# Attention stage of a routed transformer layer: queries and keys turned together, statistics in one pass, shared rotations, and PSUM places dealt anew (scores 3 to 2, side products 1 to 2)

## What is computed

```python
q, k, v = (split_heads(x @ w.T) for w in (wq, wk, wv))      # q and k also times 64 ** -0.25
q, k = rope(q), rope(k)                                      # pairs (x0, x1): x0*c - x1*s, x0*s + x1*c
out = softmax(q @ k.T + causal_mask) @ v
x1 = layernorm(x + merge_heads(out) @ wo.T)
stats = [mean, std, min, max, l2, share of |x1| < 1e-6]      # six numbers for each token
hidden = concat(x1, stats) @ r1_w.T                          # what the router reads
```

## Time and profile before

| | |
|---|---|
| time, median of 3 runs | 2268.77 us (2255.43, 2268.81, 2268.77) |
| the profiled execution, own time | 2260.15 us |
| its span (first to last instruction) | 2258.3 us |
| TensorE matmul busy | 1936.1 us (86%) |
| VectorE, ScalarE, GpSimd busy | 1347.9, 1040.6, 775.0 us |
| mean granted TensorE clock | 0.911 of 2.4 GHz |

### The profile page before, as it was taken

The page is one execution under the profiler, slowest core; times in us unless marked ns, Lnnn a source line. Parts: engine busy times, 40 slices in busy tenths (PEclk is TensorE's granted clock), DMA queues, the critical chain, the costliest instruction groups (busy, mean ns, idle before and its releaser), DMA issues. The chain is left out here.

```text
span 2258.3 us, 39106 instructions
## 1 busy us (share of the span) xinstructions
PE 1936.1 (86%) x13154; PEld 1727.6 (76%) x13154; DVE 1347.9 (60%) x3015; ACT 1040.6 (46%) x2293; POOL 775.0 (34%) x901
## 2 busy tenths in 40 slices
PE   5999999999999999999999999442178999999990
PEld 4778888878788878888878888341178999999980
DVE  7466554566654566554466663386885656656645
ACT  4344344444344444344444333315175666666655
POOL 1322043331043322033332000100085766766742
PEclk8799999999999999899999999555588999999995
DMA  4222122322223232222322221300004444554428
GB/s 121 69 75 76 47 73 70 90 76 78 60 73 78 77 84 75 62 61 61 90 80 83 64 66 27 139 34 0 0 14 128 137 156 141 155 172 133 143 50 298
DMA packets 154370, 198.48 MB, mean 88 GB/s; under 512 B 24612, under 2 KB 119824, under 8 KB 150124
## 3 DMA queue, kind: packets, MB, share of 16 engines
q1 hardware_dynamic: 138348, 186.33, 26.6%
q0 software_dynamic: 15872, 10.24, 2.7%
HBM read 129.65 MB, written 56.62 MB: 82 GB/s over the span
## 5 line engine op out<-in xcount | busy, mean ns | idle before, releaser
L518 PEld LDWEIGHTS out_ps<-v_sb,probs 128*128 128x128 f32 x4352 | 575.9, 197 | 30.6 <-ACT probs L642 7.3
L518 PE MATMUL out_ps<-v_sb,probs 128*128 128x65 f32 x4352 | 586.1, 275 | 3.6 <-ACT probs L642 3.3
L742 DVE TENSOR_REDUCE part_max<-rows_ps 128x1 f32<-128x512 f32 (+2 forms) x576 | 345.5, 617 | 204.1 <-PE rows_ps L474 137.0
L642 ACT ACTIVATE probs<-scores_ps 128x512 f32<-128x512 f32 (+3 forms) x640 | 329.7, 533 | 146.9 <-PE scores_ps L505 74.8
L1502 PE MATMUL up_ps<-xe_t,w 128*128 128x320 f32 x1920 | 289.8, 311 | 1.7 <-DVE xe_t L1609 1.7
L1502 PEld LDWEIGHTS up_ps<-xe_t,w 128*128 128x128 f32 x1920 | 284.6, 189 | 2.4 <-issue 1.9
L501 PE MATMUL scores_ps<-q,k_st 128*128 128x512 f32 (+2 forms) x640 | 279.3, 436 | 0.0
L474 PE MATMUL rows_ps<-k_st,q 128*128 128x512 f32 (+3 forms) x640 | 246.3, 408 | 25.3 <-DVE part_max L742 15.3
L896 POOL TENSOR_TENSOR products<-qk,cos_sin 128x256 f32<-128x256 f32 x224 | 160.2, 747 | 280.3 <-ACT qk L599 280.3
L502 PE MATMUL scores_ps<-q,k 68*128 68x512 f32 (+2 forms) x640 | 238.7, 373 | 0.0
L1465 POOL DMA_INDIRECT acc_rows<-out_rows,token x96 | 148.7, 1549 | 127.5 <-ACT out_rows L1592 116.5
(11 more groups left out here) (243 smaller groups left out, 2960.8 us busy)
## 6 DMA issues: line engine op xcount, KB each, us to landing
w_raw<-in_w_expert SPq DMA_DIRECT2D x32, 1536.0 KB, 6.5
k<-k_st SPq DMA_DIRECT2D x160, 128.0 KB, 2.3
q<-q_up_cols SPq DMA_DIRECT2D x128, 128.0 KB, 2.8
w_raw<-in_w_adapter SPq DMA_DIRECT2D x32, 384.0 KB, 7.1
x_t<-in_x_t SPq DMA_DIRECT2D x64, 128.0 KB, 2.3
q_up_cols<-q_st SPq DMA_DIRECT2D x64, 128.0 KB, 2.4
q_low_cols<-q_st SPq DMA_DIRECT2D x64, 128.0 KB, 2.5
x_row<-in_x SPq DMA_DIRECT2D x64, 128.0 KB, 2.1
```

Of the source, the lines that this page charges most:

```text
L518: mm = pe.matmul(o_ps[:, u % 2, s * (HD + 1):(s + 1) * (HD + 1)], probs[:, g % P_RING, s * P:(s + 1) * P], v_sb[:, place(b, j), h, :], sta ...
L642: act.activation(probs[:, g % P_RING, low:CH], s_ps[:, g % S_RING, low:CH], ACT.Exp).then_inc(exp_done, 1)
L742: red = dve.tensor_reduce(to, r_ps[:, e % 2, 0:width], AX.X, ALU.max, negate=g == 0)
```

## The change

1. **Turned together.** The host sets the rows of wq and wk side by side head by head, so that one transpose of 128 columns holds one head's query and key. Four transposes do for a tile instead of eight, with one copy (L664 in the new kernel) and one subtraction (L748). `dup` is gone, and `qt` and `kt` become one step `turn`. The halves that hold keys are moved into `k_st` by two DMAs for each tile, beside the two stores of queries; whoever reads those keys waits for the DMAs (`keys_stored`).
2. **Statistics in one pass.** The six numbers are copied to three blocks of 32 columns (GpSimd), so that upper and lower parts of data and weights meet in one matmul of 96 rows instead of three of 6 rows.
3. **Shared rotations.** In the front GpSimd makes the rotations of tiles 1, 4 and 7, VectorE the others; the split of `w_o` and `w_r1` moves behind tile 1.
4. **PSUM.** Two places for scores, two for side products; `claim` waits for the product two before. When chunks are over, side products use the places of scores and rows too, six in all.
5. **Order.** `x1` comes 3 slots after `wo`, `stats` one later, a new step `sparse` one later (the moments' first instruction moves into `x1`); rings of 4 for `y`, `x1` and the moments. Row work of units 1 to 3 moves from before the slots into slots 0 to 8. In a slot rows are sorted by unit, so a turn of maxima stands ahead of the next unit's row. The tail takes a tile each slot.

```diff
-S_RING = 3
+FIRST_ON_POOL = (1, 4, 7)
+S_RING = 2
+M_RING = 2
...
-        apart = 2 if i // GROUP == len(groups) - 1 else 7
+        apart = 1 if i // GROUP == len(groups) - 1 else 7
...
-                                  ("dup", 3, False), ("qt", 1, True), ("kt", 1, True)))
+                                  ("turn", 3, True)))
...
-        steps = (("ot", 0, True), ("wo", 2, True), ("x1", 2, False), ("stats", 0, False), ("x1t", 2, True))
+        steps = (("ot", 0, True), ("wo", 2, True), ("x1", 3, False), ("stats", 1, False), ("sparse", 1, False),
+                 ("x1t", 2, True))
...
+            def store_qk(n):
...
+                sp.wait_ge(qk_lower, n + 1)
...
                 for part_, to in enumerate(("q_up", "q_low")):
                     sp.dma_start(dram[to][:, :, n * P:(n + 1) * P].rearrange("h d t -> d h t"),
-                                 raw(q_st[0:HD, n % 2, part_])).then_inc(q_stored[n % 2], 16)
+                                 raw(parts[0:HD, n % 2, part_])).then_inc(qk_stored[n % 2], 16)
+                for part_ in range(2):
+                    sp.dma_start(raw(k_st[part_ * HD:(part_ + 1) * HD, :, cols(n)]),
+                                 raw(parts[HD:P, n % 2, part_])).then_inc(qk_stored[n % 2], 16)
...
                 if n >= 4:
-                    store_q(n - 4)
...
+                    store_qk(n - 4)
+            for u in range(HEADS):
+                load_q(u)
+                load_k2(u)
+                if u < 2:
+                    store_qk(FIRST - 2 + u)
...
-            def claim(semaphore, value):
-
-                if holder[0] is not None:
-                    pe.wait_ge(*holder[0])
-                holder[0] = (semaphore, value)
+            def claim(kind, k, semaphore, value):
+
+                n = bank_of[kind, k]
+                if holder[n] is not None:
+                    pe.wait_ge(*holder[n])
+                holder[n] = (semaphore, value)
+                return banks[n]
...
-                    three(out, lambda a: w_r1s[:, a, :], lambda b: x1_ts[:, b].rearrange("p a b -> p (a b)"),
-                          start=False).then_inc(hid_done, 1)
+                    pe.matmul(out, w_r1s[:], x1_ts[:].rearrange("p a b -> p (a b)"), start=False, stop=True)\
+                      .then_inc(hid_done, 1)
...
             for n in range(FIRST):
...
+                if n + 2 < FIRST:
+                    first_copies(n + 2)
+                if n + 4 < FIRST:
+                    upper_xt(n + 4)
+                copy_turned(r_ps[:, n % 2, :], n)
```

More of the change, by code:

```diff
@@ L93, in attention_plan @@
         begins[u] = max(slot, -1)
+    early = [("max", u, 0, s) for u in range(HEADS) for s in range(GROUP)] + [("turn", u) for u in range(HEADS)]
+    stream = [[e for e in now if e not in early] for now in stream]
     before = stream.pop(0)
-    before.sort(key=lambda e: (e[1], e[0]))
+    assert not before
+    for n, e in enumerate(early):
+        u = e[1]
+        if u == 0:
+            before.append(e)
+        else:
+            at = (0, 0, 0, 0, 2, 2, 3, 3, 5, 5, 6, 6)[n - GROUP] if e[0] == "max" else (1, 4, 8)[u - 1]
+            stream[at].append(e)
+            begins[u] = min(begins[u], at)
+    for now in stream:
+        now.sort(key=lambda e: e[1])
     ends = [first[HEADS * (k + 1)] for k in range(len(groups))]
@@ L109, in attention_plan @@
     for i in range(COUNT):
-        apart = 2 if i // GROUP == len(groups) - 1 else 7
-        late = 10 if groups[i // GROUP][1] == 3 and apart > 2 else 1
+        apart = 1 if i // GROUP == len(groups) - 1 else 7
+        late = 10 if groups[i // GROUP][1] == 3 and apart > 1 else 1
         at = max(ends[i // GROUP] + late, at + apart)
@@ L124, in attention_plan @@
     side = [[] for _ in range(length)]
-    made, taken, waiting = {}, set(), [(at, len(steps) > 6, n, 0, steps) for at, n, steps in chains]
+    made, taken, waiting = {}, set(), [(at, steps[0][0] != "ot", n, 0, steps) for at, n, steps in chains]
     while waiting:
@@ L131, in attention_plan @@
         if kind in after:
-            earlier += [x for x in [(after[kind], n - 1)] if x in every]
+            other, back = after[kind]
+            earlier += [x for x in [(other, n - back)] if x in every]
         if any(x not in made for x in earlier):
@@ L137, in attention_plan @@
         b, t = n // NT, n % NT
-        if kind in ("v", "kt") and t >= 8 and b:
+        if kind in ("v", "turn") and t >= 8 and b:
             at = max(at, ends[4 * b - 1])
-        while claims and at in taken:
+        while claims and at in taken and at < total:
             at += 1
@@ L151, in attention_plan @@
         side.pop()
-    return groups, units, chunks, first, before, stream, begins, side, made
+    bank_of, used, claimed = {}, [0, 0], {kind for _, _, steps in chains for kind, _, claims in steps if claims}
+    for g, now in enumerate(side):
+        for kind, n in now:
+            if kind in claimed:
+                late = g >= total
+                bank_of[kind, n] = used[late] % (M_RING + S_RING + R_RING if late else M_RING)
+                used[late] += 1
+    return groups, units, chunks, first, before, stream, begins, side, made, bank_of
 def attention(nc, dram, NB, NT):
-    groups, units, chunks, first, before, stream, begins, side, made = attention_plan(NB, NT)
+    groups, units, chunks, first, before, stream, begins, side, made, bank_of = attention_plan(NB, NT)
     CHUNKS = len(chunks)
@@ L585, in _ @@
             walk(main, step)
-            pe.wait_ge(*holder[0])
+            for last in holder:
+                if last is not None:
+                    pe.wait_ge(*last)
         @block.scalar
@@ L773, in step @@
             def step(kind, k):
-                r = k % 2
+                r, bank = k % ROW_RING, banks[bank_of.get((kind, k), 0)]
+                row = x1[:, r, 0:D]
                 if kind == "norm":
                     of, h = units[k]
+                    r = k % 2
                     dve.wait_ge(values_done, first[k + 1])
```

382 lines of the change are left out of this document (201 added, 181 removed).

## The result

| | time, median (range) | runs |
|---|---|---|
| before | 2262.1 us (2252.8 to 2268.81) | 4 |
| changed | 2144.0 us (2143.25 to 2145.87) | 3 |

The ratio is 0.948 [0.943, 0.954]: 118 us faster. (One more run of the changed kernel, 2444.86 us at a mean clock of 0.718, is not counted.) The forecast was 2185 with 2145 to 2240: right in sign, too small by 41 us, and the result lies just under the range, near the rival "all of it" (2138).

The account below looks back on a forecast made before the run. The slots were taken to last as long as TensorE's stream, with its idle time and half-rate clock. From 2260, terms -20 - 9 - 16 - 3 - 11 - 18 + 9 + 0 - 7 = -75 gave 2185 us, range 2145 to 2240.

Parts of the forecast that it names:

- all of it: Rival: every listed TensorE wait and all half rate goes, front gives 7, tail 10, scores cost nothing: 2138 us; chance 0.09.
- Matmuls: TensorE's stream in the slots: four fewer transposes per tile, -20 us, and two fewer statistics matmuls per tile pair, -9 us.
- Turned together: Slots: 56 tiles lose four transposes each, -20 us; copies and a low part removed from ScalarE and VectorE count nothing.
- Side places: TensorE's waits for the one side-product place go almost whole, -16 us; waits for GpSimd's statistics shrink, -3 us.
- Statistics in three steps: VectorE's block of norm and statistics, cut into pieces, no longer stops row maxima so long: -11 us (0 to -26).
- the clock: TensorE in the slots: long waits behind which it fell to 1.2 GHz go, regaining 18 of 30 us lost (0 to -30).
- the rival in which many brief stops for PSUM places throttle the clock: TensorE stops often and briefly for exponentials, time at half rate doubles, +30 instead of -18: 2233 us; chance 0.08.
- Two score places: Scores wait for the exponential of chunk g instead of g - 1: +9 us taken, near the low end of 0.
- the mechanism behind the high end: Scores wait 1.75 us for an exponential late behind ScalarE's norm wait, at all 64 tiles: +112 us; slower rival's chance 0.06.
- Front: Before the first row: a 7.41 us wait could go, but tile 3 comes later; first row near 53 us; 0 (-7 to +9).
- The ring: Front: store, landing, split, copy and low part close a chain of 6.7 us a tile, for three tiles.
- Tail: After the slots: keeping VectorE busy shortens the tail by 7 us (0 to -13).

Follow-up runs that it names:

- block: Changed kernel with row statistics and sparse share back in the norm's step, as one block in one slot; 2183.43 us, ratio 0.967.
- a second turn: Changed kernel with another claim, four transposes, copy and low part behind each tile's turn from the ninth tile on, into an unread buffer; 2161.59 us, ratio 0.956.
- s2m1: Changed kernel with two PSUM places for scores and one for side products, one bank unused; 2163.3 us, ratio 0.958.
- s3m1: Changed kernel with PSUM places as before: three for scores, one for side products; 2159.78 us, ratio 0.957.
- again_block_s3m1: Changed kernel with statistics in one block, three score places, one side place, and a whole second turn behind each tile's turn; 2248.85 us, ratio 0.995.

## Why the prediction was too small

By the traces, where the profiled execution gained 114 us and not 75, the missing 39 are these: idle time in the slots -42 for the -21 forecast (-16 - 3 - 11 + 9), clock -30 for -18, matmuls -33 for -29, and 10 us less of busy time that was not in the sum; front and tail take 8 back.

*Matmuls: right.* -29 forecast, -33 by the rows, -26 by the doubled ones.

*Turned together: the step that failed.* It said of ScalarE's copies and VectorE's low part that they "count nothing themselves" because both engines have slack. In the kernel as it stood they counted: with the block and one side place a second turn costs 56 us, some 21 of them matmuls. Beside these 21, a second claim on the only side place doubles the waits there (13.6 to 27.4 us), idle time grows by 16 or 17, and the clock loses 4 or 13 us more, by which of the two runs without it one compares. In the changed kernel, where block and single place are both gone, a second turn costs 17 to 18. Which of claim, copy and low part carries it was not separated, and no run has the second turn with only one of block and single place.

*Side places: right in size.* -19 forecast, 19 measured, and 17 with the block. But part of this is luck: half of the waits at the side place that the forecast took off here go with the second turn already (27.4 with it, 13.6 without).

*Statistics in three steps, and the clock: mechanism right, size too small.* -11 for row maxima and -18 for the clock make -29; taking the block back costs 39. In "block" the clock falls again (0.98, 25 us), in s2m1 and s3m1 hardly (the lowest stretch has 0.99), so the block alone brings back most of the clock's loss, as the prediction read from the earlier trace rows. I gave the clock back by six tenths; the rows show all of it. The Trainium skill ("TensorE: Matmul & The Clock Gate", section "A second HAM failure mode: psum-queue depth-cycling") spoke for the rival in which many brief stops for PSUM places throttle the clock. With two places its condition did not arise: the scores stop four times, 1.3 us in all, and the clock is 1.00 for 1217 us. With one place in effect the trace agrees: 324 stops of 1.06 us, and 0.69 to 0.79 in the two stretches shown.

*Two score places: +9 forecast, 3.5 measured.* The value near the low end was right; the mechanism behind the high end exists, and shows once the block is back.

*Front: 0 forecast, +6 measured.* The ring's 6.7 us came out to a tenth. Missed were GpSimd's wait for the weights ahead of its first low part (4.44 us) and VectorE's slower products beside GpSimd's rotation (3.12 us for 1.43); mending all of it gives 10 us. The pace of the front before was misread, too: the row at 43.61 in the earlier trace rows is the low part of tile 6, and that of tile 7 is at 45.72, so a tile took 3.86 us and not 3.56; this would have moved the sum by under 1 us.

*Tail: -7 forecast, -5 measured.*

Summed along one path by medians: before 2257, stats in one pass with front, tail and all that no run took back to 2249, turned together to 2193, the trade of places to 2183, the block cut to 2144. On this path the second turn gives 56 for the 20 forecast, and that is most of what was missing. The terms are not independent, so another path shares it out otherwise: the second turn costs 17 to 18 once block and single side place are gone. Block and single place do not raise each other's price (39 and 19 alone, 56 together). I had priced each stop once, by the wait that its row named. "All of it" was the nearest reading; I had given it 0.09. The new order of row work and the way of the keys by DMA were not tried by themselves; what is between again_block_s3m1 and before, 9 us, leaves little room for them.

## What to carry to other kernels

Where several in-order engines share one buffer, removing a claim and a piece of work on an engine "with slack" can win more than the bottleneck's own instructions, as long as the other obstacles stand (56 us here, and 18 without them): price it by what queues behind it, not by its engine's busy share. When TensorE idles in several stops and the clock falls after them, the stops and the clock belong together; here, where nearly all long stops went, all of the clock came back. And a second place for a result whose consumer stands behind other work was worth 875 us here, and a third almost nothing: read from the consumer's queue how late it can be.

## What was not expected of the hardware

VectorE's four products with two SBUF inputs take 1.43 us alone and 3.12 us while GpSimd makes the sums of its rotation. The Trainium skill ("SBUF — State Buffer", section "SBUF: two separate sides") says that such an instruction and a GpSimd one that reads SBUF take turns at a port that both share. The trace agrees, on both sides: one of these sums takes 0.91 us there and 0.73 alone. Sharing the rotations won nothing (2141.6 without it, 2143.4 and 2144.0 with it).

One matmul of 96 rows and 256 columns takes 0.12 us of a full stream and one of 6 rows 0.18: the few rows made nothing cheaper.
